# Eight fused sublayers on one core: TensorE adds the causal mask before the maxima are taken, and the third attention's sums stay in their PSUM bank

## What is computed

```python
x = layernorm(x + attn0(x));  x = layernorm(x + glu(x))       # causal softmax attention, int8 gated FFN
x = layernorm(x + attn1(x));  x = layernorm(x + mixture(x))   # windowed differential attention, 8 experts
x = layernorm(x + attn2(x));  x = layernorm(x + binary(x))    # causal softmax attention, binarized layer
x = layernorm(x + attn3(x));  x = layernorm(x + ternary(x))   # attention over scores * tril, ternary FFN
```

```python
att = einsum('bhqd,bhkd->bhqk', q, k) / 4
att = where(causal, -1e9, att)                  # key later than query
out = einsum('bhqk,bhkd->bhqd', softmax(att), v)
...                                             # attn3 instead:
scores = einsum('bthd,bshd->bhts', q, k) * tril # masked scores are 0, not left out
attn = softmax(scores / 16)
```

## Time and profile before

| | |
|---|---|
| median of 3 runs | 1052.92 us (1050.35 to 1055.82) |
| profiled execution, its time | 1051.1 us |
| its span, first to last instruction | 1049.4 us |
| granted TensorE clock, mean | 0.984 |
| TensorE busy | 971.5 us (93%), 6103 matmuls |
| VectorE busy | 697.7 us (66%) |
| ScalarE busy | 531.3 us (51%) |
| GpSimd busy | 334.8 us (32%) |

### The profile page before, as it was taken

The page is one execution under the profiler, slowest core; times in us unless marked ns, Lnnn a source line. Parts: engine busy times, 40 slices in busy tenths (PEclk is TensorE's granted clock), DMA queues, the critical chain, the costliest instruction groups (busy, mean ns, idle before and its releaser), DMA issues. The chain is left out here.

```text
span 1049.4 us, 16975 instructions
## 1 busy us (share of the span) xinstructions
PE 971.5 (93%) x6103; PEld 548.1 (52%) x6103; DVE 697.7 (66%) x1987; ACT 531.3 (51%) x1140; POOL 334.8 (32%) x465
## 2 busy tenths in 40 slices
PE   9999999989999989999999999999999988889896
PEld 3544454676454554433487544455556444445585
DVE  2677774687797994453323467777772788877587
ACT  4566665434888871121101567665544545655442
POOL 4211112233588861000001221112210346662452
PEclk9999999999999999999999999999999979999999
DMA  6000000100001200210000020000000000000001
GB/s 255 2 1 1 2 2 1 56 1 2 8 20 56 85 2 1 103 48 0 1 1 1 1 99 22 2 1 2 1 1 1 2 0 2 1 2 1 2 1 41
DMA packets 4823, 21.64 MB, mean 21 GB/s; under 512 B 489, under 2 KB 1769, under 8 KB 3844
## 3 DMA queue, kind: packets, MB, share of 16 engines
q1 hardware_dynamic: 4740, 20.55, 5.2%
HBM read 19.01 MB, written 1.05 MB: 19 GB/s over the span
## 5 line engine op out<-in xcount | busy, mean ns | idle before, releaser
L995 ACT ACTIVATE PB<-pair 128x1024 f32<-128x1024 f32 (+3 forms) x288 | 223.2, 811 | 137.2 <-PE pair L1780 135.9
L1255 DVE CUSTOM_DVE_ANT_0 junk<-bank,cst 128x128 bf16<-128x128 f32 (+3 forms) x384 | 171.1, 487 | 106.1 <-PE bank L1764 103.9
L826 POOL TENSOR_SCALAR_AFFINE_SELECT PB<-PB 128x256 f32<-128x256 f32 x192 | 78.8, 413 | 309.0 <-ACT PB L995 307.5
L1258 DVE TENSOR_REDUCE pmx<-bank 128x1 f32<-128x512 f32 x192 | 122.5, 684 | 40.6 <-PE bank L1764 39.8
L1764 PE MATMUL bank<-KO_r,QO_r 64*128 64x512 f32 (+3 forms) x576 | 139.9, 412 | 9.5 <-DVE A L1333 5.2
L1798 PE MATMUL pvb<-PB,V 128*32 128x512 f32 (+3 forms) x1152 | 123.2, 499 | 10.5 <-ACT PB L995 8.4
L1764 PEld LDWEIGHTS bank<-KO_r,QO_r 64*128 64x128 f32 x576 | 72.3, 187 | 105.4 <-DVE pmx L1255 40.6
L1776 PE MATMUL pair<-QO_r,KO_r 64*128 64x512 f32 (+3 forms) x576 | 115.2, 391 | 12.6 <-ACT PB L995 10.8
L832 POOL TENSOR_TENSOR parts_r<-y_f,parts_r 128x512 fp32r<-128x512 f32 x24 | 30.8, 1284 | 279.1 <-ACT parts_r L966 279.1
L1780 PE MATMUL pair<-ms,sel_r 64*128 64x512 f32 (+3 forms) x576 | 101.4, 345 | 0.0
L1066 ACT ACTIVATE KO<-pair,nm 128x128 f32<-128x128 f32 x256 | 90.1, 392 | 9.7 <-DVE nm L1478 9.3
(11 more groups left out here) (237 smaller groups left out, 1696.2 us busy)
## 6 DMA issues: line engine op xcount, KB each, us to landing
WF<-in_moe_gu SPq DMA_DIRECT2D x1, 3520.0 KB, 12.4
WF<-in_tern_w SPq DMA_DIRECT2D x1, 3072.0 KB, 10.2
WA<-in_w_att SPq DMA_DIRECT2D x2, 1024.0 KB, 10.4
V<-in_moe_d SPq DMA_DIRECT2D x1, 1792.0 KB, 7.3
xT<-in_xT SPq DMA_DIRECT2D x2, 512.0 KB, 5.8
WA<-in_w_att SPq DMA_DIRECT2D x2, 512.0 KB, 7.2
X<-in_x SPq DMA_DIRECT2D x1, 1024.0 KB, 10.8
A<-in_rope SPq DMA_DIRECT2D x1, 1024.0 KB, 4.8
```

Of the source, the lines that this page charges most:

```text
L826: pool.affine_select(p2, p2, pattern=[[0, 2], [1, P]], compare_op=ALU.is_ge, fill=0.0, base=0, channel_multiplier=-1).then_inc(causal, 1)
L995: act.activation(pb[:, st % 2, 2 * i:2 * i + 2, 0:n], ps[:, :, 0:n], ACT.Exp, scale=scale)\
L1255: r_done(dve.tensor_tensor_reduce(junk[:, (r_used - 1) % 3, 0:n], ps[:, 0:n], tri[:, HALF - n:HALF], 1.0, LOWEST, ALU.add, ALU.max, accum_ ...
L1258: r_done(dve.tensor_reduce(to, ps[:, 0:n], AX.X, ALU.max))
```

## The change

TensorE adds the mask by matmuls of the identity with a bf16 copy of the mask's last 128 columns (`trib`), into the bank that holds the scores, before VectorE reads it. VectorE takes plain maxima of all blocks. The two banks of an item are now both asked for before its first matmul. In the third attention the last sum is written back into its PSUM bank, and the product with 1/sum reads it there.

```diff
+        trib = sb("trib", [P, P], BF16)
...
                 act.wait_ge(ld_cst, 16)
                 act.activation(idb[:, :], idf, ACT.Copy).then_inc(cast_ready, 1)
+                act.activation(trib[:, :], tri[:, HALF - P:HALF], ACT.Copy).then_inc(tri_ready, 1)
...
-                if (t + 1) * P - c * HALF <= HALF:
-                    r_done(dve.tensor_tensor_reduce(junk[:, (r_used - 1) % 3, 0:n], ps[:, 0:n], tri[:, HALF - n:HALF], 1.0, LOWEST,
-                                                    ALU.add, ALU.max, accum_out=to))
-                else:
-                    r_done(dve.tensor_reduce(to, ps[:, 0:n], AX.X, ALU.max))
+                r_done(dve.tensor_reduce(to, ps[:, 0:n], AX.X, ALU.max))
...
-                            step(dve.tensor_tensor(num, ps[:, :, :, 0:HD], num, ALU.add))
-                            r_done(dve.tensor_tensor(o, num, wide, ALU.mult))
+                            step(dve.tensor_tensor(ps[:, :, :, 0:HD], ps[:, :, :, 0:HD], num, ALU.add))
+                            r_done(dve.tensor_tensor(o, ps[:, :, :, 0:HD], wide, ALU.mult))
...
+                        diagonal = (t + 1) * P - c * HALF <= HALF
+                        slots = [r_slot() for _ in range(TWO)]
                         for j in range(TWO):
                             rows = slice(j * ROWS, (j + 1) * ROWS)
-                            pe.matmul(r_slot()[:, 0:n], qd[rows, TWO * g + i, t * P:(t + 1) * P],
-                                      kd[rows, TWO * g + i, c * HALF:c * HALF + n], start=True, stop=True).then_inc(r_full, 1)
+                            last = pe.matmul(slots[j][:, 0:n], qd[rows, TWO * g + i, t * P:(t + 1) * P],
+                                             kd[rows, TWO * g + i, c * HALF:c * HALF + n], start=True, stop=not diagonal)
+                            if not diagonal:
+                                last.then_inc(r_full, 1)
+                        if diagonal:
+                            pe.wait_ge(tri_ready, 1)
+                            for j in range(TWO):
+                                pe.matmul(slots[j][:, n - P:n], idb[:, :], trib[:, :], start=False, stop=True).then_inc(r_full, 1)
```

More of the change, by code:

```diff
@@ L694, in build @@
         cast_ready = sem("cast_ready")
+        tri_ready = sem("tri_ready")
         glu_ready = sem("glu_ready")
```

## The result

The changed kernel took 1114.3 us (median of 6, 1111.5 to 1120.1), beside 1055.4 for the kernel before in the same runs. The ratio is 1.0575, with a 95% interval of 1.054 to 1.0609. Slower was right, and 1090 was 24 us too little; the time lies just inside the range. The increase is 1.6 times the one forecast.

The account below looks back on a forecast made before the run. In the attentions the other engines wait for TensorE, which bounds them. Masks +40.6, mask copy +1.2, VectorE's reads -1.2 and sums -3.1 gave +37.5 us on 1052.9, so 1090; the 8-in-10 range was 1066 to 1116.

Parts of the forecast that it names:

- the masks: TensorE's mask matmuls in 192 diagonal items of the causal attentions: 58 us more work, 40.6 of it on the path.
- The shares that land (85%, a half, a fifth): Parts of the mask cost reaching the path: ahead of scores 28.9 us, of another maximum 3.9, of pv 2.1.
- VectorE gains next to nothing: Plain for masked maxima on VectorE: same rate, 1.2 us off for accumulator reads at the ends of 24 stages.
- the sums: Third attention's line 1333, one operand now in PSUM: three slow operations should take 0.42 us, 3.1 us off.
- the start: First mask matmul waits for ScalarE's copy of the mask, TensorE standing from 15.3 to some 16.7: 1.2 us.
- Both banks first ... Nothing taken: Both bank waits ahead of an item's first matmul: pair ends as before, 0 us; a mask might idle VectorE 0.2.
- no term for the clock: The sum of terms over the whole kernel, +37.5 us, held none for TensorE's clock.
- the second rival: Masks also hold up VectorE's banks, then TensorE's next pair: all 58 us land plus 13, 1112 to 1127; chance 0.17.

Follow-up runs that it names:

- e3_no_mask_own_bank: The changed kernel without the mask matmuls and with each score matmul waiting for its own bank only: 1046.8 us, ratio 0.9937 to the kernel before.
- e2_no_mask: The changed kernel without the mask matmuls, both banks still asked for first: 1062.8 us, ratio 1.0108 to the kernel before.
- the square: Changed kernel with or without masks, own or both banks, each with and without zero-matmul fillers: -6.6 to 60.6 us more than the kernel before.

## Why the prediction was right and wrong

**Right: the masks.** The sum had 40.6 us for them; with the clock held they are 37.1 and 40.3. The prices stand in the trace: 0.40 for an item ahead of scores, 0.31 from 256-column scores to the mask (0.11 + 0.11 + 0.10), and the changes of shape each way. The shares that land (85%, a half, a fifth) were guesses, and no run tests them one by one; that their sum fits may be luck in part. The Trainium skill (page TensorEngine Tiling (Array Packing), section Key Properties) says that a change of tiling mode drains TensorE. The trace agrees, at 0.20 us of an item; the run in the scores' own shape was 19 us faster, some 7 of which may be the clock's.

**Right: VectorE gains next to nothing**, and the sums 3.4 us for 3.1. GpSimd's operation of line 843 stood beside the other two long products as well (839.76 and 926.42 for 839.88 and 926.49). The run with neither masks nor the joint wait took 6.6 us less in all, so plain maxima would be worth some 3 us. That is not shown: the intervals leave it open, the run leaves out the mask, and its clock was higher (0.988 for 0.984).

**Right: the start.** The first mask waited for the copy until 17.04, behind a pair at 15.46; 1.26 us idle are put down to it. The clock's part in it had no term: half clock followed from 17.9 to 24.7, 6.8 us, where the kernel before had it from 16.3 to 19.7.

```profile
15.46 0.33 PE L1765 MATMUL bank<-KO_r,QO_r 64*128 64x128 f32 x2
...
17.04 0.28 PE L1772 MATMUL bank<-trib,idb 128*128 128x128 bf16 x2 [1.26 <-ACT trib L940]
```

**Wrong: "Both banks first ... Nothing taken".** This step failed by its mechanism. I argued from the pair, which ends when it did. The price is in what follows: of three banks one is left for VectorE to read while two are filled, so in a run of maxima the engines take turns. It is 5 to 8 us at a held clock and 13 to 18 without. The prediction named the mask as what could leave VectorE idle there; the turns come without any mask. It also read TensorE's waits for VectorE from the matmuls alone (9.5 us before line 1764). The weight loads of the same line had waited 40.6 + 25.1 us for VectorE's banks, so the matmuls were often let in by VectorE:

```profile
L1764 PEld LDWEIGHTS bank<-KO_r,QO_r 64*128 64x128 f32 x576 | 72.3, 187 | 105.4 <-DVE pmx L1255 40.6 <-DVE pmx L1258 25.1 <-issue 20.1
```

With own banks that wait stays what it was, 66.0 us, 0.8 at the longest (e3_no_mask_own_bank); with both banks it is 105.0 and up to 2.4 (e2_no_mask):

```profile
PEld bank L1766 <- DVE pmx L1257: 66.0, 124, 0.8
```

```profile
PEld bank L1765 <- DVE pmx L1257: 105.0, 181, 2.4
```

**Wrong: no term for the clock.** This is the larger failed step. The sum put the clock at nothing without a word on it: all prices were taken at the full clock. But with the masks, and with the joint wait, TensorE stood at half clock for longer (the windows above), at waits such as those of 0.84 us before 60.54 and 1.95 us before 892.75. The profile before had the sign: 0.94 in the third attention, against 0.99 and 1.00. That is 22 of the 60 us by the square, 14 to 27 by the bounds.

Both steps together are some 28 us, more than the 23 by which the sum fell short. The range held the time by 2 us, and its upper end was there for the second rival, which was not the cause.

**The second rival** had the time (1112 to 1127) and part of the way: TensorE's next pair waiting for VectorE with all that is queued behind. It held the mask for the reason, its 13 us came from there, and it let all 58 us of the masks land, where 37 to 40 did. So its time was right by luck.

Together, from the runs: 38 us masks, 6 the joint wait, 22 the clock, less 6.6 for the plain maxima and the sums: 59.4 of 60.6. That they add up is no proof, since all but the rounding comes from the same square.

What stays open is how much of the 22 us the fillers' own cost makes, and whether each part of the clock's share can be put down to one of the waits. The masks and the joint wait bring it on each alone: without fillers the one costs 9 to 18 us more than with them, the other 5 to 13.

## What to carry to other kernels

A term moved from an engine that waits to the one that is waited for costs most of its price (here some 38 of 58 us), though it frees nothing where it came from, and on TensorE a small matmul of another shape also costs what stands around it: here 0.13 us of matmuls, ahead of scores, made 0.4. Ask for the buffers of a group one by one where a ring has few of them; with two of three taken at once, producer and consumer take turns, and then a low clock, which own banks hid in the one run of maxima looked at, lengthens each turn (1.64 us for 1.34). When a change adds waits to TensorE, look at its granted clock in the windows of before, and give the clock a term of its own. The row maximum of a softmax need not be masked at all if the scores it takes in are of the same size: that version, with own banks and the sums in their bank, was the fastest here (ratio 0.9937), though half of what it gained is the sums'.

## What the runs showed of the hardware that I had not expected

- Zero matmuls put into TensorE's waits, 44 in 22 places, made a kernel 14 us faster in spite of their own time, with the clock at 0.989 for 0.964. In kernels whose mean clock was 0.984 and 0.988 the same fillers did not raise it and cost 6 to 8 us.
- The Trainium skill (page TensorE: Matmul & The Clock Gate, section HAM oscillation — how this bites in real kernels) says that waits between bursts of matmuls, there for transfers, bring the clock down again. The trace agrees for waits for another engine's banks, at 0.50 from 891.7 to 908.8.
- Two bf16 matmuls of 128 columns with weights of their own stood 0.066 us apart at full clock (938.604 and 938.670), not 0.055; in 64-row shape four of them, side by side for two banks, took 0.10 us.
- The accumulator read of the masked maximum was free: from one 512-column maximum to the next it is 0.61 us with it (845.20 to 845.81 in the kernel before) and 0.60 without.
